# Gathers of four features for 32 batch rows each instead of one feature for 128 rows, gram released by chunk, and gathers paced from the tenth chunk of 16

## The reference

```python
e = jnp.stack([tbl_f[ids[:, f]] for f in range(26)], axis=1)      # 512 x 26 x 128
combined = jnp.concatenate([dense[:, None, :], e], axis=1)        # 512 x 27 x 128
inter = jnp.einsum('bfd,bgd->bfg', combined, combined)
z = jnp.concatenate([dense, inter[:, iu, ju]], axis=1)            # iu, ju: pairs above the diagonal
h = jnp.concatenate([z, dense], axis=1)
h = jnp.maximum(h @ W_top1 + b_top1, 0.0)                         # 607 -> 512
h = jnp.maximum(h @ W_top2 + b_top2, 0.0)                         # 512 -> 256
y = h @ W_top3                                                    # 256 -> 1
```

## Time and profile before

| | us |
|---|---|
| timed, median of 3 | 138.34 (137.31 to 138.55) |
| profiled execution, span | 161.6 |
| TensorE busy in it | 113.8 (70%) |
| VectorE | 85.1 (53%) |
| ScalarE | 65.7 (41%) |
| GpSimd | 71.7 (44%) |

### The profile page before, as it was taken

How to read it: one execution, slowest core, us unless ns; L and a number is a source line. 1 busy time by engine, 2 the same in 40 slices (tenths; PEclk the granted TensorE clock), 3 DMA queues, 4 the chain that set the end, 5 groups by cost and what they waited for, 6 DMA issues and landing times.

```text
span 161.6 us, 1858 instructions
## 1 busy us (share of the span) xinstructions
PE 113.8 (70%) x674; PEld 98.9 (61%) x674; DVE 85.1 (53%) x162; ACT 65.7 (41%) x109; POOL 71.7 (44%) x72
## 2 busy tenths in 40 slices
PE   5499996995980997580000798762999697944994
PEld 5378774884860885570000897761999666943992
DVE  5399989997896370010000648966055731365031
ACT  3286994894894050200000657362133341332112
POOL 2687787878778777777770055710000000000000
PEclk9999999999998589967555569999699999996599
DMA  4998974797396221122110001110000000000000
GB/s 108 234 370 322 253 252 119 214 232 209 88 398 227 62 56 49 49 54 60 49 49 16 0 16 49 41 28 0 0 0 4 0 0 0 4 0 0 0 0 1
DMA packets 6331, 14.59 MB, mean 90 GB/s; under 512 B 1842, under 2 KB 2354, under 8 KB 6195
## 3 DMA queue, kind: packets, MB, share of 16 engines
q1 hardware_dynamic: 4130, 10.23, 20.4%
q0 software_dynamic: 2048, 4.20, 9.7%
q10 hardware_dynamic: 144, 0.05, 0.2%
HBM read 14.47 MB, written 0.00 MB: 90 GB/s over the span
## 4 chain that ended last, share of the span: by engine, by line
PE 34%; POOL 21%; issue 13%; another core or an unknown queue 11%; DVE 9%; DMA 6%; ACT 4%; DVEq 0%; ACTq 0%
POOL e_rows L345 21%; PE gram L413 15%; PE late L453 8%; DMA e_rows<-in_tbl,idx 3%; DMA idx<-in_ids_rows 2%; PE look L395 2%; DVE flip L748 2%; DVE flat L750 2%; ACT pT_hi L561 2%; PE late L385 2%; PE look L474 1%; PE late L386 1%; DVE dots L543 1%; ACT dots L561 1%
## 5 line engine op out<-in xcount | busy, mean ns | idle before, releaser
L345 POOL DMA_INDIRECT e_rows<-in_tbl,idx x64 | 70.8, 1107 | 33.0 <-issue 18.6
L413 PE MATMUL gram<-eT 128*123 128x108 f32 x256 | 32.9, 294 | 23.0 <-DVE dots L543 19.3
L413 PEld LDWEIGHTS gram<-eT 128*123 128x123 f32 x256 | 32.1, 210 | 23.8 <-ACT dots L561 17.9
L385 PE MATMUL late<-onehot,table_hi 128*128 128x512 f32 x84 | 35.3, 420 | 4.0 <-DVE table_lo L684 2.4
L691 DVE TENSOR_SCALAR onehot<-ids,row_of_partition 128x512 fp32r<-128x512 int32 x72 | 30.4, 483 | 7.5 <-PE late L386 5.8
L386 PE MATMUL late<-onehot,table_lo 128*128 128x512 f32 x84 | 34.1, 406 | 0.0
L543 DVE COPY dots<-gram 32x216 f32<-32x216 f32 (+1 forms) x32 | 12.3, 384 | 30.9 <-remote 18.3
L561 ACT ACTIVATE dots<-gram 32x216 f32<-32x216 f32 x32 | 10.9, 340 | 40.2 <-remote 22.2
L385 PEld LDWEIGHTS late<-onehot,table_hi 128*128 128x128 f32 x84 | 16.6, 198 | 8.4 <-ACT table_hi L561 2.7
L386 PEld LDWEIGHTS late<-onehot,table_lo 128*128 128x128 f32 x84 | 16.7, 198 | 3.2
L395 PE MATMUL look<-ident,e_rows 128*128 128x128 f32 x64 | 10.7, 294 | 6.7 <-DMA e_rows<-in_tbl,idx 6.3
(11 more groups left out here) (51 smaller groups left out, 110.2 us busy)
## 6 DMA issues: line engine op xcount, KB each, us to landing
table<-in_tbl SPq DMA_DIRECT2D x7, 512.0 KB
ids<-in_ids_bcast SPq DMA_DIRECT2D x10, 256.0 KB
table<-in_tbl SPq DMA_DIRECT2D x2, 640.0 KB
w_raw<-in_w SPq DMA_DIRECT2D x1, 1280.0 KB
e_rows<-in_tbl,idx POOLq DMA_INDIRECT x64
table<-in_tbl SPq DMA_DIRECT2D x2, 256.0 KB, 5.7
w_raw<-in_w SPq DMA_DIRECT2D x1, 512.0 KB
x_rows<-in_dense SPq DMA_DIRECT2D x1, 256.0 KB
```

What stands on the lines that cost most here:

```text
L345: pool.indirect_dma_start(out=e_rows[:, n % GROUPS_AHEAD, s % GROUP, :], out_offset=None, in_=tables[f][:, :], in_offset=bass.IndirectOffs ...
L385: pe.matmul(bank, table_hi[0:KP, i % 2, c, :], hot, start=c == 0, stop=False)
L413: last = pe.matmul(gram[0:ROWS_OUT, n % 2, q, 0:QUADS * NG_COL], eT_flat[:, b * SLOTS:b * SLOTS + ROWS_OUT], eT[:, b:b + QUADS, 0:NG_COL], ...
```

## The change

Three things.

1. A gather now reads four tables for 32 batch rows, not one table for 128. The 16 gathered tables lie one behind another in one array, and the index is the row's id plus the table's start; the two parts come in by DMA and VectorE adds them before the first gather. Group c, made of four such gathers, holds all 16 gathered features of chunk c, and its copy writes 16 neighbouring slots of 32 batch rows.
2. Gram is issued by chunks, each of which needs only its own group and those before. The orders of TensorE, ScalarE and VectorE are written anew: pair turns, layer 1 and looks stand between chunks, layer 2 of the first half moves behind the last chunk, no group follows tables 0 and 6, and layer 3 takes a bank of `look`.
3. From chunk `PACED_FROM = 9` on (counted from 0; gathers 36 to 63) a gather waits until the gather `IN_FLIGHT = 2` before it has landed. Each gather has a semaphore of a ring of 20.

```diff
-GROUP, GROUPS_AHEAD = 4, 5
+GROUPS_AHEAD = 5
+UNIT = 32
+PACED_FROM, IN_FLIGHT = 9, 2
+NCK = B // UNIT
+PER_GATHER = P // UNIT
+GROUP = NG // PER_GATHER
...
+AFTER_TABLE = {1: 0, 2: 1, 3: 2, 4: 3, 5: 4, 7: 5, 8: 6, 9: 7}
+LOOK_ORDER = [("dense",)] + [("group", c) for c in AFTER_TABLE.values()]
+LOOK_ORDER += [("group", 8), ("group", 9), ("turn", 0), ("group", 10), ("group", 11), ("turn", 1)]
...
-            pool.wait_ge(idx_in, 16)
-            for t, g in ALL_GROUPS:
-                n = t * NGR + g
-                if n >= GROUPS_AHEAD:
-                    wait_look_full(pool, ("group", *ALL_GROUPS[n - GROUPS_AHEAD]))
-                for s in GROUPS[g]:
-                    f = GATHERED[s]
+            pool.wait_ge(idx_ready, 1)
+            for c in range(NCK):
+                if c >= GROUPS_AHEAD:
+                    wait_look_full(pool, ("group", c - GROUPS_AHEAD))
+                for k in range(GROUP):
+                    n = c * GROUP + k
+                    if c >= PACED_FROM:
+                        before = n - IN_FLIGHT
+                        pool.wait_ge(gather_in[before % len(gather_in)], 16 * (before // len(gather_in) + 1))
                     pool.indirect_dma_start(
-                        out=e_rows[:, n % GROUPS_AHEAD, s % GROUP, :], out_offset=None, in_=tables[f][:, :],
-                        in_offset=bass.IndirectOffsetOnAxis(ap=idx[:, t, f:f + 1], axis=0)
-                    ).then_inc(rows_in[t][g], 16)
+                        out=e_rows[:, c % GROUPS_AHEAD, k, :], out_offset=None, in_=gathered[:, :],
+                        in_offset=bass.IndirectOffsetOnAxis(ap=idx[:, n:n + 1], axis=0)
+                    ).then_inc(gather_in[n % len(gather_in)], 16)
...
-            def gram_tile(t):
+            def gram_chunk(n):
-                upto = LOOK["group", t, NGR - 1]
+                upto = LOOK["group", n]
...
+            dve.wait_ge(idx_in, 16)
+            dve.tensor_tensor(idx[:, :], idx_parts[:, 0, :], idx_parts[:, 1, :], ALU.add).then_inc(idx_ready, 1)
...
+                copy(eT[:, c * UNIT:(c + 1) * UNIT, 1:1 + NG],
+                     look[:, LOOK[what] % 2, :].rearrange("d (f b) -> d b f", f=NG)).then_inc(done, 1)
```

```diff
+            dots_chunk(0)
+            w_split(0)
+            dots_chunk(1)
+            w_split(1)
+            group(8)
...
+            flip_tile(0)
+            for n in (4, 5, 6):
+                dots_chunk(n)
+                w_split(n)
+            turn_lo(0)
...
+            flip_tile(1)
+            group(10)
+            dots_chunk(8)
...
+            dots_chunk(11)
+            flip_tile(2)
+            h1_rest(0)
+            group(12)
+            dots_chunk(12)
+            turn_lo(2)
+            dots_chunk(13)
+            group(14)
+            dots_chunk(14)
+            dots_chunk(15)
+            flip_tile(3)
```

## The result

The changed kernel took 126.42 us, median of 4 runs (124.42 to 127.87), against 138.44 (137.31 to 138.66) of the kernel before in runs beside it: a ratio of 0.9085, 95% interval 0.898 to 0.9189. Five further rounds on another chip gave a median of 129.33 us and a ratio of 0.9209 (0.9129 to 0.9289). So the forecast of 122 us was right in direction and in its range (117 to 130), and 4.4 us too low, against the second median 7.3. A ratio here leaves out disturbed runs, which a median keeps; where the two say different sizes, both are given.

A forecast was written before the change was run, and what follows sets the result against it. TensorE's order, not the gathers, was taken to bound gram and layers. Gram start 57.7 + work 40.3 + waits 7.0 = 105.0; plus tail 15.7 = 120.7; plus 0.9 = 121.6, forecast 122 us, range 117 to 130.

The forecast's parts named there:

- The base: Kernel before on a time axis without the late message: gram from 64.4, end at 138.3 us; 0.9 added to reach the median.
- 22.5 us hold: Start of gram in the recorded run: chunk 0's done message came late, shifting later work 22.5 us; taken as that run's own.
- The sum of 120.7: Whole changed kernel: chunk 15's end at 105.0 plus 15.7 for the tail; with 0.9 added, 121.6 us.
- Shape of the gathers, index sum: Group copies kept at 0.72 us each; one VectorE add before the first gather shifts every gather by 0.3 us.
- Pacing: GpSimd's gathers from chunk 9: the one two ahead lands in time, 0.3 us to spare, cost 0; group 15 in at 96.1.
- Rival D: GpSimd, gathers 36 to 63: pacing throttles, period is half the landing time; 158 us at a landing of 5.47; chance 0.05.
- Table stage: Tables before gram: the new group order cuts TensorE's wait for group 6 to 0.8; gram starts at 57.7, not 64.4: -6.7 us.
- rival C: Table stage gains nothing: landings of groups 6 and 7 slip, wait and low clock return; +3 to +6, 125 to 128; chance 0.10.
- Gram: Gram by chunks, from 57.7: 40.3 us of TensorE work plus 7.0 of waits, so chunk 15 ends at 105.0.
- Rival A: Gram stage: waits longer than walked, small lateness handed on, clock drops with them; up to 9 us, 126 to 131; chance 0.22.
- Tail: After the last chunk: 15.7 us instead of 18.2, layer 2 of half 0 filling the flip wait, pairs at full clock.
- Rival B: End of gram: gathers slowed beside flips bind, group 15 at 104; 123 us, or 125 with a tail of 18.3; chance 0.08.

The follow-up runs named there:

- the repeated run: The kernel before once more, unchanged, for a profile of a usual execution: 137.41 us, span 135.7.
- late looks: Kernel before with the change's table-stage order alone, looks 8, 9 and 10 behind gram chunks 1, 5 and 7: 132.41 us, ratio 0.9667.
- the early ones: Kernel before with the change's table-stage order alone, looks 8, 9 and 10 behind gram chunks 1, 2 and 5: 137.75 us, ratio 1.0037.
- the unpaced kernel with the better order: Changed kernel without pacing, six places moved so that copies gram waits for stand ahead of flips and rests: 120.43 us, ratio 0.8777.

## Why the prediction was right, and what in it was wrong

1. *The base.* That the 22.5 us hold is not the kernel's was right, by the repeated run. The axis without it ended at 138.3, and a run without a hold has a span of 135.7: time is span plus 1.7 to 2.0 in every run. The sum of 120.7 was a span, so 2 belonged to it and not 0.9.

2. *Shape of the gathers, index sum.* Copies 0.69 (VectorE) and 0.63 (ScalarE) against 0.72 expected, and the first gather starts at 4.85 and not later than before (4.89): nothing, as said.

3. *Pacing.* This is **the step that failed**: "the wait is met with 0.3 us to spare, cost 0". The landing was taken as the end of traffic, 2.0 to 2.2 us; who waits starts 2.7 to 2.8 after the issue. Group 15 was expected in by 96.1 and its last row was turned at 105.90. Of the 8.0 us by which gathers are drawn out some 2.4 reach the end of gram, since TensorE would not have turned that group before 104.15 anyway. Rival D's formula (group 15 in at 60.1 + 13.5 L + L) with L = 2.75 gives 100.0; the rest is the first gather of each group, the late landing of gather 42 and a start 0.6 us later. Rival D had the mechanism; the forecast gave it nothing, because L was read from the wrong row. That so little of it reached the end is luck in part: by the walk as forecast look 15 comes at 102, and the paced rows would have held it up by 4 us.

4. *Table stage.* Gram was forecast at 57.7 and started at 56.5, in other runs with this order at 56.8 to 61.9. -6.7 was forecast, 7.3 came in this pair, and some 5 on average. The late looks in the kernel before gave 4.6 to 5.5 us of the time alone, with no other part of the change. It stays only if the next looks are late enough: the early ones gave all back. That is rival C's mechanism, one place further on, and the change's order avoids it.

5. *Gram.* Forecast 47.3 us, measured 53.6. Unpaced the stage takes 49.9 (57.84 to 107.72), so 2.6 of the miss are the walk and 3.7 stand between the paced and the unpaced execution. The walk: 1.9 of waits (1.5 before chunk 6 against 0.5, 1.9 before chunk 10 against 1.2 and before 13 against 1.4, 0.2 of the 0.5 at looks; those before 12, 14 and 15 were right), and 0.7 of work. Of that work 0.2 is a slip: 36 matmuls at the prediction's own 39 in 4.9 us are 4.5, not 4.3, and 4.5 was measured. The 3.7: the paced kernel started gram 1.3 earlier and lost this lead, 0.6 of it at look 8, whose gathers are not paced, the rest at look 11, whose gathers are; 2.4 are the last look's wait and the last chunk at low clock. Rival A, small lateness handed on, is the walk's part in a mild form, without the loss of clock that it feared. Its price was too small as well: half of the 40 us of work at 3.61 for 1.78 would add up to 20 us, not 9.

6. *Tail.* 15.7 forecast, 15.8 measured, with the pair part in 4.57 us at full clock (before: 6.67); it was 6.62 again in the repeated run. All nine profiled executions of the changed kernel and its variants have a tail of 15.8. Layer 2 now fills TensorE's wait for the flip. That this is what keeps the clock was not tried alone.

7. *Rival B* counted on locked ports beside the flips. Gathers beside the copy into `flat` were not longer: 68.43 lies across it (0.88 us) and takes 0.95. Gathers are longer elsewhere, mostly in the table stage (see below).

With 120.7 + 2.0 for the base, +6.3 for gram, -1.2 for the earlier start and 0.1 for the tail one gets 127.9, the profiled run's own 127.87. The forecast was near because its gains of 7 us in placement and 2.5 in the tail were right; the gram stage, from which it wanted another 7.5 (54.8 on its axis to 47.3), gave 0.1 with the pacing (53.7 to 53.6), 3.8 without it, and 6.9 (46.8) in the unpaced kernel with the better order.

## What to carry to other kernels

Price a wait on a DMA by when a waiter in the trace last started after such a DMA's issue, not by the end of its traffic: 0.8 us between traffic's end and waiter, some more at each group's first gather, made 8 us over 28 gathers, even if other work hides it today. A cost that hides behind an in-order engine's list is paid as soon as that list is shortened, so test a throttle again after each reordering. When a look, copy or load is moved out of a full stage, check that where it goes the data has already come, or the stage in front gives the gain back with interest in lost clock.

## What the runs showed of the hardware that was not expected

**GpSimd and VectorE.** In the changed and in the unpaced kernel three gathers each are longer than 0.95 us between 60 and 70 us. All six start inside a VectorE operation of 0.69 us that reads two operands from SBUF (L761). GpSimd's timeline of the changed kernel, first one from the table stage:

```profile
12.50 1.28 POOL L341 DMA_INDIRECT e_rows<-in_gathered,idx  x1 [0.30 <-issue]
...
61.96 1.17 POOL L341 DMA_INDIRECT e_rows<-in_gathered,idx  x1 [0.30 <-issue]
...
68.43 0.95 POOL L341 DMA_INDIRECT e_rows<-in_gathered,idx  x1 [0.31 <-issue]
...
74.71 0.95 POOL L341 DMA_INDIRECT e_rows<-in_gathered,idx  x1 [2.52 <-DMA e_rows<-in_gathered,idx]
```

and VectorE's, the operation that each of these starts in:

```profile
11.60 2.46 DVE L708 TENSOR_SCALAR onehot<-ids,row_of_partition 128x512 fp32r<-128x512 int32 x6
...
61.62 0.69 DVE L761 TENSOR_TENSOR table_lo<-w_raw,w_hi 128x512 fp32r<-128x512 f32 x1
...
68.32 0.88 DVE L770 COPY flat<-flip 128x702 f32<-128x702 f32 x1
...
74.60 0.87 DVE L779 TENSOR_TENSOR pT_lo<-look,pT_hi 126x384 fp32r<-126x384 f32 x1 [0.47 <-ACT pT_hi L565]
```

What was left of L761's operation at the gather's start (0.35 us here; 0.64 and 0.49 for those at 64.94 and 66.81) less 0.13 is what the gather takes over its 0.95 (0.22, 0.51, 0.36). Inside the mask at 12.50 a gather takes 1.28. Inside the copy into `flat` at 68.32 it is not longer, nor inside the operation at 74.60, one of whose two inputs (`look`) is in PSUM. The traces of all 14 executions say the same of gathers that start in such an operation more than 0.15 us before its end: in `flat` (29 gathers) and beside two inputs of which one is in PSUM (40) none takes over 0.97 us; beside two inputs of 512 or more elements in SBUF all 151 take 0.98 or more, and beside the masks 168 of 177.

The Trainium skill ("SBUF — State Buffer", Who interferes with whom) has a VectorE operation with two inputs in SBUF contend with a GpSimd instruction that reads SBUF, and copies and the masks' kind of operation (tensor_scalar) hold the lock when they run in the two-port mode. The rows agree on the first. On the second the masks agree, and `flat` does not contradict it: a mask writes 512 elements in 0.41 us, 0.80 ns each, `flat` 702 in 0.88, 1.25 ns each, so it seems to run in the slower mode; the mode itself stands in no trace. The 0.35 us copy into `band` (364 elements) did make the two gathers longer that started in it more than 0.15 us before its end: 1.00 and 1.07.

This is worth most in the table stage, where TensorE waits for rows: the first 36 gathers of the changed kernel take 1.23 us on average, not 0.94. An estimate from these two numbers is 10 us of GpSimd's time, in the chain that bounds the reordered kernel. No run tried to win it back.

**Executions differ by more than the change.** One of before had a hold that cost 22.5 us, in which a finished chunk's message did not arrive; one of before with the pacing ran at a mean clock of 0.667 with a span of 157.9; one timed run of before took 358.16 us where the others beside it took 137 to 140. The cause of none was found. A single profiled execution must be set beside the timed runs before its waits are read.
